# Causal mask folded into the row maxima by GpSimd, one more slot of lag, and a reordered router in a fused attention and expert kernel

## The reference

```
h      = layernorm(x)
q,k,v  = h @ Wq + bq, ctx @ Wk + bk, ctx @ Wv + bv          (per head, 16 wide)
s      = where(key <= query, q.k / 4, -inf)
x      = x + tanh(g_xattn) * (softmax(s) @ v @ Wo + bo)
h      = layernorm(x)
logits = h @ Wr + br;   kept = the two largest
x      = x + tanh(g_ffn) * sum over kept experts of softmax(logits)[e] * (gelu(h @ W1[e] + b1[e]) @ W2[e] + b2[e])
```

## Time and profile before

| | |
|---|---|
| median of 3 runs | 941.34 us (938.75 to 942.17) |
| profiled execution | 942.84 us, span 940.9 us |
| PE / DVE / ACT / POOL busy over the span | 90 / 64 / 47 / 27% |
| attention stage | about 34 to 468 us of the span |
| first expert tile starts | 483 us |

### The profile page before, as it was taken

The page is one execution under the profiler, slowest core; times in us unless marked ns, Lnnn a source line. Parts: engine busy times, 40 slices in busy tenths (PEclk is TensorE's granted clock), DMA queues, the critical chain, the costliest instruction groups (busy, mean ns, idle before and its releaser), DMA issues. The chain is left out here.

```text
span 940.9 us, 24425 instructions
## 1 busy us (share of the span) xinstructions
PE 846.5 (90%) x7600; PEld 750.5 (80%) x7601; DVE 600.4 (64%) x1521; ACT 442.3 (47%) x962; POOL 257.6 (27%) x239
## 2 busy tenths in 40 slices
PE   3599999999999999999539999999999999999990
PEld 2488888888888888888338789998989998989980
DVE  2357888888888888887636555555555555555540
ACT  2155555655555555654224444554444455544440
POOL 3001333222332333323210322232332232223332
PEclk9699999999999999999659999999999999999996
DMA  8765666665667787864388432323233233322222
GB/s 185 141 135 132 158 152 129 139 155 156 155 159 202 188 185 176 174 164 156 130 288 295 87 53 48 54 53 53 48 50 52 48 59 50 51 48 36 30 24 25
DMA packets 87944, 108.77 MB, mean 116 GB/s; under 512 B 12832, under 2 KB 81568, under 8 KB 85664
## 3 DMA queue, kind: packets, MB, share of 16 engines
q1 hardware_dynamic: 72448, 87.17, 37.4%
q0 software_dynamic: 14304, 19.15, 12.7%
q10 hardware_dynamic: 1088, 1.11, 0.4%
HBM read 46.82 MB, written 34.36 MB: 86 GB/s over the span
## 5 line engine op out<-in xcount | busy, mean ns | idle before, releaser
L1220 POOL DMA_INDIRECT out_rows<-yg,xs x78 | 126.6, 1624 | 332.7 <-ACT yg L1262 190.3
L1352 PE MATMUL bank<-xh,wts 128*128 128x256 f16 x1872 | 214.2, 275 | 0.0
L1368 PE MATMUL bank<-wts,hh 128*128 x1872 | 210.6, 273 | 0.0
L1352 PEld LDWEIGHTS bank<-xh,wts 128*128 x1872 | 185.0, 99 | 22.5
L1368 PEld LDWEIGHTS bank<-wts,hh 128*128 128x128 f16 x1872 | 183.2, 98 | 21.2
L1252 ACT ACTIVATE hf<-bank,b1t,gscale 128x256 f32<-128x256 f32 x312 | 154.7, 562 | 24.3 <-PE bank L1352 24.3
L979 PE MATMUL bank<-va,probs 128*128 128x102 f32 x1024 | 139.7, 278 | 8.1 <-DVE ao L696 8.1
L979 PEld LDWEIGHTS bank<-va,probs 128*128 128x128 f32 x1024 | 124.2, 192 | 10.7 <-DVE ao L696 6.2
L1262 ACT ACTIVATE yg<-yb,xs 128x256 f32<-128x256 f32 x78 | 35.4, 500 | 199.5 <-DVE yb L1301 199.5
L583 ACT ACTIVATE probs<-bank 128x512 f32<-128x512 f32 x128 | 76.9, 601 | 101.8 <-PE bank L962 95.2
L1291 DVE SCALAR_TENSOR_TENSOR hh<-hf,hscale,hh 128x512 f16<-128x512 f32 x156 | 117.1, 751 | 5.6
(11 more groups left out here) (169 smaller groups left out, 1082.0 us busy)
## 6 DMA issues: line engine op xcount, KB each, us to landing
wts<-in_W SPq DMA_DIRECT2D x16, 1024.0 KB, 7.9
wts<-keys SPq DMA_DIRECT2D x96, 128.0 KB
wts<-queries SPq DMA_DIRECT2D x96, 128.0 KB
xs<-token_rows SPq DMA_DIRECT2D x39, 272.0 KB
split_weights<-wts SPq DMA_DIRECT2D x8, 1024.0 KB, 4.6
wts<-split_weights SPq DMA_DIRECT2D x8, 1024.0 KB
xin<-in_x SPq DMA_DIRECT2D x16, 256.0 KB, 4.0
cin<-in_ctx_in SPq DMA_DIRECT2D x16, 256.0 KB, 4.2
```

The lines of the kernel that those rows point to most:

```text
L1220: pool.indirect_dma_start(out=out[:, :], out_offset=bass.IndirectOffsetOnAxis(ap=numbers, axis=0), in_=yg[m % 2][:, half, :], in_offset=No ...
L1352: last = pe.matmul(HB[c // 2][:, c % 2 * TILE:(c % 2 + 1) * TILE], wts[:, bass.ds(expert[1], 1), at:at + P], xh[b][:, xp, k, :], start=q = ...
L1368: last = pe.matmul(YB[b][:, half * D:(half + 1) * D], hh[b][:, hp, c, half * P:(half + 1) * P], wts[:, bass.ds(expert[0], 1), at:at + D], ...
```

## The change

- `maskT` and `ident16` are gone, and the matmul of 512 columns with them. In their place POOL writes, for each quad, a tile `cover` (128 queries by 4 heads by 128 keys, bf16) with one `affine_select`: the row maximum where key <= query and +1e30 where not. There are four such tiles; they lie in the space of `first_xs`, which is otherwise filled at the end of the stage.
- ST takes `cover` as the stationary operand in place of the broadcast `rowmax`, per head one matmul with `negident` and one with the scores.
- ST is done two slots after S (quad n - 2) and no longer one; ACT's exponential moves with it. PV stays at three slots (quad n - 3).
- DVE's reduction waits for `cover_ready` of two quads back, not for ST.
- POOL: in slots 1 and 5 the root comes first and the select behind it; `xb` moves from slot 5 to slot 6; the scatters go from slots 4 to 7 to slots 3, 4, 5 and 7.
- PE, slot 7: the router products and the total of the weight's squares stand ahead of PV instead of at the slot's end. The router's moving operand is repeated eight times (64 columns for 8), and `ALLSUM` lies behind it.
- DVE: the f32 mask of the router is dropped (`msk16` serves), `wscale` is not written per group but worked out from `wsquares` in the table at the stage's end (four small instructions), and in slot 1 `rest` moves behind `norm2` and the token placing.

```diff
+        cover = [env["first_xs"][i // 2][:, :, :].rearrange("p h r -> p (h r)")[:, 256 * (i % 2):256 * (i % 2) + 256]
+                 .bitcast(BF16).rearrange("p (a k) -> p a k", a=4) for i in range(4)]
...
@@ POOL, it()
+                        if there(g):
+                            pool.wait_ge(max_ready, g * QUADS + n + 1)
+                            settled(pool)
+                            when(pool, n >= 4 or there(g - 1), st_psum, g * QUADS + n - 3)
+                            settled(pool)
+                            pool.affine_select(out=cover[n % 4][:, :, :],
+                                               in_=rowmax[n % 2][:, :].unsqueeze(2).to_broadcast([P, 4, P]),
+                                               compare_op=ALU.is_ge, fill=MASKED, base=0, pattern=[[0, 4], [-1, P]],
+                                               channel_multiplier=1).then_inc(cover_ready, 1)
-                        if n == 5 and there(g + 1):
+                        if n == 6 and there(g + 1):
...
-                        if n >= 4 and there(g - 2):
-                            b, r = (n - 4) // 2, n % 2
+                        if n in (3, 4, 5, 7) and there(g - 2):
+                            b, r = divmod((3, 4, 5, 7).index(n), 2)
@@ ACT, it()
-                        q, pg = (QUADS - 1, g - 1) if n == 0 else (n - 1, g)
+                        q, pg = (QUADS + n - 2, g - 1) if n < 2 else (n - 2, g)
@@ DVE, it()
-                            when(dve, n >= 2 or there(g - 1), st_psum, g * QUADS + n - 1)
+                            when(dve, n >= 2 or there(g - 1), cover_ready, g * QUADS + n - 1)
...
-                            dve.wait_ge(w_scaled, g)
-                            dve.tensor_copy(wscale[:, p1, bass.ds(e, 1)], wnow[:, p1:p1 + 1])
-                            step(dve.tensor_copy(wsquares[:, p1, bass.ds(e, 1)], wsum[:, p1:p1 + 1]))
-                        if n == 1 and there(g1):
-                            rest(g1, n)
+                            step.later(dve.tensor_copy(wsquares[:, p1, bass.ds(e, 1)], wsum[:, p1:p1 + 1]))
... (norm2 and the token placing, msk replaced by msk16)
+                        if n == 1 and there(g1):
+                            rest(g1, n)
@@ PE, it()
-                            tg, m, i = (g, n - 1, par) if n >= 1 else (g - 1, QUADS - 1, p1)
+                            tg, m, i = (g, n - 2, par) if n >= 2 else (g - 1, QUADS + n - 2, p1)
-                            pe.wait_ge(max_ready, tg * QUADS + m + 1)
+                            pe.wait_ge(cover_ready, tg * QUADS + m + 1)
-                            pe.matmul(ps[:, :], ident16[:, :], maskT[:, :].unsqueeze(1).to_broadcast([P, 4, P]),
-                                      start=True, stop=False)
-                            for a in range(4):
-                                pe.matmul(ps[:, a * P:(a + 1) * P], rowmax[m % 2][:, a:a + 1].to_broadcast([P, P]),
-                                          negident[:, :], start=False, stop=False)
                             for a in range(4):
                                 h = 4 * (m % 4) + a
+                                pe.matmul(ps[:, a * P:(a + 1) * P], cover[m % 4][:, a, :],
+                                          negident[:, :], start=True, stop=False)
                                 last = pe.matmul(ps[:, a * P:(a + 1) * P], kst[i][:, h, tok],
-                                                 qst[i][:, h, tok], start=False, stop=a == 3)
+                                                 qst[i][:, h, tok], start=False, stop=True)
+                        if n == 7 and there(g - 1):
+                            pe.wait_ge(x2T_ready, g * GT)
+                            for b in range(GT):
+                                last = product(PJA[:, b * MANY * E:(b + 1) * MANY * E],
+                                               lambda k: x2T[:, k, b * P:(b + 1) * P],
+                                               lambda k: wr[:, k, :].unsqueeze(1).to_broadcast([P, MANY, E]))
+                            last.then_inc(r_psum, 1)
... (and the total of the squares; both go from the end of slot 7 to this place, between ST and PV)
```

More of the change, by code:

```diff
@@ L31 @@
 EPS = 1e-5
-MASKED = -1e30
+MASKED = 1e30
 SPAN = 4
@@ L127, in bass_flamingo @@
         negident = sb("negident", [P, P], BF16)
-        ident16 = sb("ident16", [P, P], BF16)
-        qsteps, ksteps, maskT = (sb(name, [P, P], BF16) for name in ("qsteps", "ksteps", "maskT"))
+        qsteps, ksteps = (sb(name, [P, P], BF16) for name in ("qsteps", "ksteps"))
         earlier = sb("earlier", [P, P], BF16)
@@ L177, in attention_and_routing @@
     (x, ctx_in, g_xattn, g_ffn, w_q, b_q, w_k, b_k, w_v, b_v, w_o, b_o, W1, b1, W2, Wr, br, out,
[L178 removed]
+     xs_dram, w_dram, bank, qst, kst, qfull, kfull, ident, negident, qsteps, ksteps, earlier, ones16, rank1,
      rank0, ones8, region0, base, mostsel, tgx, tgf, gates_in, power, wscale, wsquares, padrow,
@@ L450, in _ @@
                 step.later(pool.memset(ksteps[:, :], -FUTURE / STEP))
-                step.later(pool.memset(maskT[:, :], 0.0))
                 step.later(pool.memset(earlier[:, :], 1.0))
@@ L656, in _ @@
                 step.later(dve.tensor_copy(base[:, :], ints[:, 2, :]))
-                step.later(dve.tensor_scalar(negident[:, :], ident[:, :], -1.0, None, ALU.mult))
-                dve.tensor_copy(ident16[:, :], ident[:, :]).then_inc(dve_consts, 1)
+                dve.tensor_scalar(negident[:, :], ident[:, :], -1.0, None, ALU.mult).then_inc(dve_consts, 1)
                 step.wait()
@@ L785, in it @@
                             dve.wait_ge(ex_ready, g - 1)
-                            step(dve.tensor_tensor(em[:, :, :], ex[:, :, :], msk[:, :, :], ALU.mult))
+                            step(dve.tensor_tensor(em[:, :, :], ex[:, :, :], msk16[:, :, :], ALU.mult))
                             for b in range(GT):
-                                step.later(dve.tensor_tensor_scan(cnt[:, b, :], ones8[:, :], msk[:, b, :], 0.0,
+                                step.later(dve.tensor_tensor_scan(cnt[:, b, :], ones8[:, :], msk16[:, b, :], 0.0,
                                                                   ALU.mult, ALU.add))
@@ L791, in it @@
                             step.later(dve.reciprocal(erec[:, :], esum[:, :]))
-                            step.later(dve.tensor_tensor(cm[:, :, :], cnt[:, :, :], msk[:, :, :], ALU.mult))
+                            step.later(dve.tensor_tensor(cm[:, :, :], cnt[:, :, :], msk16[:, :, :], ALU.mult))
                             step(dve.tensor_tensor(mostsel[:, :], mostsel[:, :], cnt[:, :, E - 1], ALU.max))
@@ L855, in it @@
                             step(last)
-                            step.later(dve.tensor_tensor(msk[:, :, :], lg[:, :, :],
-                                                         mx[:, :, 1:2].to_broadcast([P, GT, E]), ALU.is_ge))
                             dve.tensor_tensor(msk16[:, :, :], lg[:, :, :],
@@ L964, in it @@
                             last.then_inc(st_psum, 1)
+                        if n == 7 and (there(g - 1) or there(g)):
+                            when(pe, there(g1), q_left, g1 + 1)
+                            when(pe, there(g - 2), pos_read, g - 1)
+                            when(pe, there(g - 1), x2_ready, g * GT)
+                        if n == 7 and there(g - 1):
[5 more added lines that the diff above has]
+                            last.then_inc(r_psum, 1)
@@ L965, in it @@
+                        if n == 7 and there(g):
+                            pe.wait_ge(w_sums, g * 4 + 4)
+                            pe.matmul(ALLSUM, ones8[:, 0:1].to_broadcast([P, P]), partsum[:, :],
+                                      start=True, stop=True).then_inc(w_total, 1)
                         if there(g if n >= 3 else g - 1):
@@ L1004, in it @@
                             product(PJB[:, 0:D], lambda k: aoT[1][:, k, :], lambda k: wo[:, k, :]).then_inc(o_psum, 1)
-                        if n == 7 and (there(g - 1) or there(g)):
-                            when(pe, there(g1), q_left, g1 + 1)
-                            when(pe, there(g - 2), pos_read, g - 1)
-                            when(pe, there(g - 1), x2_ready, g * GT)
-                        if n == 7 and there(g - 1):
-                            pe.wait_ge(x2T_ready, g * GT)
-                            for b in range(GT):
-                                last = product(PJA[:, b * E:(b + 1) * E], lambda k: x2T[:, k, b * P:(b + 1) * P],
-                                               lambda k: wr[:, k, :])
-                            last.then_inc(r_psum, 1)
-                        if n == 7 and there(g):
-                            pe.wait_ge(w_sums, g * 4 + 4)
-                            pe.matmul(ALLSUM, ones8[:, 0:1].to_broadcast([P, P]), partsum[:, :],
-                                      start=True, stop=True).then_inc(w_total, 1)
                 loop_over_groups(pe, it)
```

(3 more changed lines are left out.)

21 lines of the change are left out of this document (9 added, 12 removed).

## The result

The changed kernel takes **946.07 us** (median of 9 runs, 940.41 to 949.27), the kernel before 940.85 beside it (9 runs): ratio 1.007, interval 1.0046 to 1.0093. It is slower by 0.7%; the forecast was 929. The value lies inside the stated range (911 to 949), but on the other side of no change. The profiled execution took 949.09 us (span 947.2), against 942.84 before.

What follows compares the result with a forecast made beforehand. PE was taken as the bound, DVE close behind. About -0.9 us a group (period 26.33 to 25.45) gave 12.6 over 14 groups, 13 with fill, drain and lag: 929 us, range 911 to 949.

Steps and rivals of the forecast that it cites:

- Mask matmul and selects: PE regains 0.21 us per mask matmul, 0.85 a group in slots 1 to 4; each POOL select takes 0.8 us.
- What the select does to DVE: Deciding step: POOL selects stretch DVE instructions with two SBUF inputs; priced slot by slot, PSUM reads expected to pass.
- 6 and 7: Slots 6 and 7: `xb` behind the select meets DVE's second split; 0.5 us late a group (0 to 1.5).
- My row on POOL: Slots 6 and 7: select then `xb`, 0.8 + 1.26 = 2.06 us from the end of the split.
- slots 5 to 7 and slot 0: Per-group terms where DVE leads: -0.4 us for slots 5 to 7, +0.1 for slot 0.
- the router's move: Slot 7, router ahead of PV: fills PE's wait for the normalisation and gains 0.25 us a group, not 1.2.
- The rival of the clock: Shorter PE work and more waits bring the steady part's clock to 0.94; 950 us, chance 0.05.
- The scatters: On POOL they stand behind a waiting select; only the root was said to be awaited soon; no cost given.
- The sum: About -0.9 us a group, 12.6 over 14 groups; with fill, drain and lag 13, giving 929.8 for the profiled execution.
- Eight times the columns: The router's moving operand at 64 columns in place of 8 on PE: costs nothing.
- The lag: Exponentials have one slot less before PV: 0.2 us of PE wait a group, plus about 1 us once at the end.
- The shared access decides: Rival: every select stops a DVE instruction for its full 0.8 us; 965 us, partly true 946 to 955; chance 0.14.

Runs made afterwards that it cites:

- e1: Changed kernel with `xb` on POOL cut to 8 of 256 columns, the rest zero: 930.75 us, ratio 0.9907 to the kernel before.
- e3: Changed kernel with `xb` moved from slot 6 to slot 7, behind the select there: 931.66 us, ratio 0.9904 to the kernel before.
- e12: Changed kernel with selects writing only 8 of 128 keys a head, `xb` still full in slot 6: 921.36 us, ratio 0.98 to the kernel before.
- e4: Changed kernel with the scatters in slots 3, 3, 4 and 5, `xb` as changed: 943.23 us, ratio 1.0021 to the kernel before.
- e2: Changed kernel with `xb` back in slot 5, behind the select there: 941.73 us, ratio 1.0009 to the kernel before.
- e6: e5 with the router and the total of squares put back to the end of slot 7: 934.42 us, ratio 0.9935 to the kernel before.
- e10: e5 with one slot of lag again between the maxima and the second matmuls: 957.27 us, ratio 1.0186 to the kernel before.
- e15: e5 with the quads of slots 6 and 7 masked on TensorE again, `xb` staying in slot 7: 940.32 us, ratio 1.0011 to the kernel before.
- e5: Changed kernel with `xb` in slot 7 behind the select and the scatters in slots 3, 3, 4 and 5: 928.68 us, ratio 0.9872 to the kernel before.
- e7: e5 with the router's weights streamed once (8 columns, not 64): 930.85 us, ratio 0.9884 to the kernel before.
- e16: e5 measured once more, nothing changed: 929.79 us, ratio 0.9903 to the kernel before.
- e8: e5 with selects writing only 8 of 128 keys a head, the rest of the cover constant: 914.49 us, ratio 0.9719 to the kernel before.
- e9: The kernel before with `xb` in slot 7 in place of slot 5, nothing else: 939.16 us, ratio 0.9973.
- e13: e5 with the quads of slots 6 and 7 masked on TensorE again and `xb` behind slot 6's maxima: 933.10 us, ratio 0.9929 to the kernel before.
- e18: e5 with `xb` last in slot 7, behind the root for the next `xn`: 923.40 us, ratio 0.9843 to the kernel before.

## Why the prediction was wrong, step by step

- *Mask matmul and selects.* The select takes 0.81 us on POOL, as taken (0.8). PE did get its time back where it leads: that part of the period fell from 14.47 to about 13.65 us, 0.8 for the 0.85 counted. (The 14.63 of the prediction are the mean period less the stretch of one group, 11.70, which is the shortest; the mean stretch is 11.83.)
- *What the select does to DVE: this is the step that failed.* It read: "6 and 7: `xb` now follows the select ... I take 0.5 (0 to 1.5)". The clash of the split measured 2.23 - 0.74 = 1.5 us in ten of twelve groups, the upper bound. My row on POOL, 0.8 + 1.26 "from the end of the split", left out the scatter of slot 5 ahead of it: it ends at 214.05, 0.9 us behind the end of the first split (213.14), so select and `xb` both come late and both lie on the second split. The trace of the kernel before already had such a scatter, stretched beside `third`:

```profile
211.52 1.49 POOL L512 DMA_INDIRECT token_rows<-pay,slots  x1 [0.18 <-issue]
```

  e1 (-1.66 us a group), e3 (-1.27) and e12 (-1.97) each break this row in another way, and each takes the loss away.
- *What the clash costs by itself.* At a clock of 1.00 the stretch is 12.03 us with it, 0.2 over the kernel before, where the forecast had 0.3 less (slots 5 to 7 and slot 0). That is 0.5 us a group, and such groups have a period of 25.6 us where nothing else comes in. By these groups it alone would not have made the kernel slower.
- *What followed from it and was not in the sum: the clock.* PE waits 1.36 us where the forecast had the router's move gain 0.25, and in six of twelve groups the clock then fell to 0.50 and the stretch grew by another 1.4 us. With the drain this is the largest term. The rival of the clock had this mechanism with a chance of 0.05 and in the wrong place; its 950 us are nearer to the measured 946.07 than the forecast. The runs tie it to the wait: e1, e3 and e12, where PE waits 0.9 us at most ahead of the output product, have no such stretch in 36 groups; the changed kernel and e4 have 9 in the 20 groups with the full clash and its wait of 1.2 to 1.6 us, and none in the 4 with the small one. Why it comes behind one such wait and not behind the next is open. A shorter or another wait can have it too (e2, e6, e10 and e15, one or two groups each).
- *The scatters were not priced.* The prediction named them as standing behind the select, but gave no cost for the fourth, in slot 7 behind `xb`. It costs 6.9 us of drain in the trace (e4), and 0.5% between the ratios of e4 and of the change (intervals just apart, 1.0043 and 1.0046).
- *The sum.* The profiled execution is 19.3 us over its forecast (949.09 for 929.8). Over twelve groups the stretch is 13.4 us over the forecast, 8.3 by the clock and 5.1 by the clash, and the rest of the period 0.4 under it; the drain is 7.8 longer where some 0.5 less was forecast; the experts' stage is 1.8 shorter. These add up to 19.5.
- *The router.* 0.25 us a group was taken. The difference of the periods of e5 and e6 is just that, but by luck: it is one group at the lower clock, and the others show nothing. Eight times the columns: nothing taken, nothing measured (e7).
- *The lag.* Its price (0.2) was small indeed: PE waits for exponentials 1.4 us in 300 in e5 and 2.9 in e16. That it is what makes the selects possible at all (e10) the prediction assumed without a number.
- *The rivals.* "The shared access decides" had the right cause of the clash. It put the price on every select, 0.8 each, 6.4 a group. DVE is busy 180.80 of 210.60 us, 22.7 a group, 1.8 over the 20.9 that the prediction counted without selects, and 1.5 of it is the one split: the reductions and the other PSUM instructions let most selects through. Shrinking all eight selects in e5 (e8) gives 1.15 us a group, 0.14 each. By the rule of the Trainium skill cited in the prediction (SBUF — State Buffer) the holder keeps the shared pair for its whole instruction; the trace agrees, and shows that a waiting DVE instruction can lose to two of POOL's in turn (2.23 us).

With the row broken and the scatters early, a kernel with the time of the forecast exists: e5 and e16 take 928.7 and 929.8 us at a period of 25.6, against 929 and 25.45. Its parts fit less well than the total: in e5 the stretch is 11.4 us on the mean where the forecast had 11.5, but the rest of the period 14.3 where it had 13.9. The order of POOL's queue, and what a gap of PE does to its clock, were not thought through.

## What to carry to other kernels

When work moves to GpSimd, draw up its queue and VectorE's side by side for one period and look at what VectorE runs beside each GpSimd instruction: what reads PSUM passes, what has two SBUF inputs or is a `tensor_scalar` on SBUF stands still. Two GpSimd instructions in a row cost nearly their sum (1.5 us here), and taking one away can drop the next on a worse victim (e9, e13), so place the long one where the other engine waits or reads PSUM (e18). Before a clash gets a price, read the period group by group, with the granted clock beside it: here the mean of 26.44 us hid groups of 25.6 and of 27.0. And for each DMA that is moved, ask who waits for its landing in the last groups, where nothing hides it.

## What the runs showed that I had not expected

A `tensor_scalar` on 128x2 elements takes 0.68 us for 0.17 when `xb` holds the pair (e5): the length of the victim does not matter. Scatters issued by GpSimd suffer too: 1.50 us for 1.0 beside a split (212.55 in the changed kernel's trace), and the kernel before had two such in a group (211.52 and 214.58, 1.49 us each). The lower clock comes behind a gap of only 1.5 us, lasts while PE is full again (138 to 140 us: 2.00 busy at 0.50), and stays away behind an equal gap elsewhere (235.84 to 247.81 us: 1.00). The nine executions of the changed kernel, 940.41 to 949.27 us, go with it: the mean clock of the whole execution is 0.953 in the fastest and 0.943 in the slowest.
